# Broadcast of the expert combine weights: high and low part in the input products' one-pass format, in place of three bf16 parts

## What is computed

```python
g = jax.nn.sigmoid(xf @ gate_w.T)
topv, topi = jax.lax.top_k(g, K)                     # K = 4 of E = 16 experts
wn = topv / jnp.sum(topv, axis=-1, keepdims=True)
combine = jnp.zeros_like(g).at[jnp.arange(T)[:, None], topi].add(wn)
hin = jnp.einsum('td,edh->eth', xf, e_win)           # h = 64 per expert
vin = jnp.einsum('td,edh->eth', xf, e_vin)
h = silu(hin) * vin * combine.T[:, :, None]
routed = jnp.einsum('eth,ehd->td', h, e_wout)
shared = silu(xf @ ws_in) * (xf @ vs_in) @ ws_out
```

## Time and profile before

| | us |
|---|---|
| median of 3 runs | 918.67 |
| lowest, highest | 916.25, 920.44 |
| the profiled execution | 916.93 |
| its span | 915.2 |
| broadcast products, L1392: 128 | 49.4 busy, 386 ns each |
| transposes of the weights, L1382: 64 | 6.6 busy, 227 ns each |

### The profile page before, as it was taken

How to read it: one execution, slowest core, us unless ns; L and a number is a source line. 1 busy time by engine, 2 the same in 40 slices (tenths; PEclk the granted TensorE clock), 3 DMA queues, 4 the chain that set the end, 5 groups by cost and what they waited for, 6 DMA issues and landing times.

```text
span 915.2 us, 17726 instructions
## 1 busy us (share of the span) xinstructions
PE 823.2 (90%) x5783; PEld 643.9 (70%) x5783; DVE 669.4 (73%) x1759; ACT 363.3 (40%) x621; POOL 372.1 (41%) x372
## 2 busy tenths in 40 slices
PE   6879866799999999899989999999999999999966
PEld 5646655677777777777777777777777777777754
DVE  5899944577777777777786878777867777878654
ACT  4767742224343434333333443333434343433131
POOL 5040037253536262626262626353726353534200
PEclk8999977699999999999999999999999999999979
DMA  4877734300403040404030403040304040400000
GB/s 114 258 242 271 272 116 119 115 25 24 126 23 126 24 126 23 126 23 126 23 126 23 126 23 126 23 126 23 126 23 126 23 126 23 126 23 24 1 11 12
DMA packets 53104, 81.01 MB, mean 89 GB/s; under 512 B 10176, under 2 KB 36952, under 8 KB 49112
## 3 DMA queue, kind: packets, MB, share of 16 engines
q1 hardware_dynamic: 53080, 80.68, 28.2%
HBM read 55.24 MB, written 25.43 MB: 88 GB/s over the span
## 4 chain that ended last, share of the span: by engine, by line
PE 49%; DVE 17%; issue 14%; DMA 10%; POOL 5%; SPq 3%; ACT 2%; POOLq 1%; DVEq 0%; ACTq 0%
PE bank L1402 12%; DMA max_b<-max_scratch 7%; PE bank L1372 5%; PE bank L1376 5%; PE bank L1373 5%; PE bank L1392 4%; PE bank L1345 3%; DVE st L991 3%; PE bank L1321 3%; DVE acc L839 2%; PE bank L1319 2%; DVE Y L1003 2%; PE bank L1326 2%; DMA x_in<-in_L_attn_x_dram 2%; DVE out_sb L1003 2%
## 5 line engine op out<-in xcount | busy, mean ns | idle before, releaser
L755 ACT ACTIVATE s_in<-bank 128x512 f32<-128x512 f32 x144 | 85.9, 597 | 195.9 <-PE bank L1376 195.0
L1402 PE MATMUL bank<-ewout,h 128*128 128x128 f32 x1024 | 146.5, 286 | 0.0
L1402 PEld LDWEIGHTS bank<-ewout,h 128*128 128x128 f32 x1024 | 123.9, 191 | 25.4 <-issue 25.4
L554 POOL TENSOR_TENSOR rs<-ve,half 128x4 f32<-128x4 f32 x32 | 32.6, 1019 | 267.5 <-DVE ve L999 267.5
L1103 DVE TENSOR_TENSOR h<-s_in,bank 128x512 f32<-128x512 f32 x144 | 98.1, 681 | 58.5 <-PE bank L1376 50.3
L1372 PE MATMUL bank<-yT_hi,in_hi 128*128 128x512 f32 x288 | 128.2, 445 | 6.8 <-DVE h L1103 6.8
L1376 PE MATMUL bank<-yT_lo,in_hi 128*128 128x512 f32 x288 | 115.3, 400 | 0.0
L1373 PE MATMUL bank<-yT_hi,in_lo 128*128 128x512 f32 x288 | 114.6, 398 | 0.0
L540 POOL TENSOR_TENSOR D<-a_tok,max_b 128x512 f32<-128x512 f32 x64 | 65.4, 1043 | 118.5 <-DVE max_b L911 67.9
L1107 DVE TENSOR_TENSOR h<-h,bank 128x512 f32<-128x512 f32 x128 | 87.3, 682 | 19.8 <-PE bank L1392 19.8
L952 DVE TENSOR_TENSOR state<-kept,bank 64x130 f32<-64x130 f32 x128 | 36.6, 286 | 64.8 <-POOL kept L569 34.7
(11 more groups left out here) (197 smaller groups left out, 1634.2 us busy)
## 6 DMA issues: line engine op xcount, KB each, us to landing
xact_scratch<-xact SPq DMA_DIRECT2D x16, 1024.0 KB, 4.9
max_b<-max_scratch SPq DMA_DIRECT2D x15, 1024.0 KB, 7.7
xa<-xact_scratch SPq DMA_DIRECT2D x16, 512.0 KB, 6.4
silu_z<-xact_scratch SPq DMA_DIRECT2D x16, 512.0 KB, 3.8
inter_w<-inter_scratch SPq DMA_DIRECT2D x30, 256.0 KB, 7.0
x_in<-in_L_attn_x_dram SPq DMA_DIRECT2D x16, 256.0 KB, 4.9
xt_scratch<-x_t SPq DMA_DIRECT2D x16, 256.0 KB, 4.8
xT<-xt_scratch SPq DMA_DIRECT2D x16, 256.0 KB, 8.0
```

The costliest lines, as they stand in the source:

```text
L755: act.activation(s_in[:, j % 2], bank[4][:], ACT.Silu).then_inc(silu_done, 1)
L1402: i = pe.matmul(bank[7][:, k * P:(k + 1) * P], h2[:, j % 2, k * P:(k + 1) * P], w, start=(j == k == 0), stop=(j == NJ), skip_group_check=True)
```

## The change

The combine weights are split into two parts in fp32r, a high part and the rest (`comb2`: 16 + 16 columns for each chunk), in place of three in bf16. VectorE's five operations of part 3 become two: a cast and a subtraction. The transposes take `comb2` in fp32, 32 columns, and fill 32 partitions of bank 6 over all of its 512 columns. `combT` is fp32r with 128 partitions: ScalarE fills the first 32 in each pass, after a new wait for the last broadcast of the pass before, and the rest is set to zero once. `pair_rows` is fp32r with 128 rows, made in `pair_f` (two parts for three) and copied. The broadcast product is so an fp32r product on the full 128x128 array. `ident_bf` goes; the counts of the semaphores follow.

```diff
-        pair_rows = sb("pair_rows", [3 * NX, NJ, P], BF16)
+        pair_rows = sb("pair_rows", [P, NJ, P], F32R)
-        comb_r = sb("comb_r", [P, 2, NC, NX])
-        comb3 = sb("comb3", [P, NC, P // NX, NX], BF16)
-        combT = sb("combT", [3 * NX, G], BF16)
+        comb2 = sb("comb2", [P, NC, 2 * NX], F32R)
+        combT = sb("combT", [P, G], F32R)
...
-            halves = pair_rows[:].rearrange("r j (t m) -> r j t m", t=P // HX)
-            for part in range(3):
+            halves = pair_f[:].rearrange("r j (t m) -> r j t m", t=P // HX)
+            for part in range(2):
                 pool.affine_select(out=halves, in_=halves, compare_op=ALU.not_equal, fill=1.0, base=-NX * part,
                                    pattern=[[-2, NJ], [-1, 2], [0, HX]], channel_multiplier=1).then_inc(pool_const, 1)
                 pool.wait_ge(pool_const, CONSTS + 1 + part)
+            pool.tensor_copy(pair_rows[:], pair_f[:]).then_inc(pool_const, 1)
...
-            pool.memset(comb3[:], 0.0).then_inc(phase2_const, 1)
+            pool.memset(combT[:].bitcast(F32), 0.0).then_inc(phase2_const, 1)
...
                     act.wait_ge(combT_mm, f + 1)
-                    copy(combT[:], bank[6][0:3 * NX, 0:G // 2].bitcast(BF16)).then_inc(combT_out, 1)
+                    prev(act, bc_mm, f, NJ)
+                    copy(combT[0:2 * NX], bank[6][0:2 * NX, :]).then_inc(combT_out, 1)
...
                     after(9)
-                    dve.tensor_copy(comb3[:, :, 0], comb[:]).then_inc(route, 1)
+                    dve.tensor_copy(comb2[:, :, 0:NX], comb[:]).then_inc(route, 1)
                     after(10)
-                    dve.tensor_tensor(comb_r[:, 0], comb[:], comb3[:, :, 0], ALU.subtract).then_inc(route, 1)
-                    after(11)
-                    dve.tensor_copy(comb3[:, :, 1], comb_r[:, 0]).then_inc(route, 1)
-                    after(12)
-                    dve.tensor_tensor(comb_r[:, 1], comb_r[:, 0], comb3[:, :, 1], ALU.subtract).then_inc(route, 1)
-                    after(13)
-                    dve.tensor_copy(comb3[:, :, 2], comb_r[:, 1]).then_inc(route, 1)
+                    dve.tensor_tensor(comb2[:, :, NX:], comb[:], comb2[:, :, 0:NX].bitcast(F32), ALU.subtract
+                                      ).then_inc(route, 1)
...
                 for k in range(NC):
-                    i = pe.transpose(bank[6][:, k * P // 2:(k + 1) * P // 2].bitcast(BF16),
-                                     comb3[:, k].rearrange("p t e -> p (t e)"), ident_bf[:])
+                    i = pe.transpose(bank[6][0:2 * NX, k * P:(k + 1) * P], comb2[:, k].bitcast(F32), ident[:])
                 i.then_inc(combT_mm, 1)
```

More of the change, by code:

```diff
@@ L89, in mixer_moe_block @@
         ident = sb("ident", [P, P])
-        ident_bf = sb("ident_bf", [P, P], BF16)
         block_mask = sb("block_mask", [P, P])
         center = sb("center", [P, P])
-        pair_rows = sb("pair_rows", [3 * NX, NJ, P], BF16)
+        pair_rows = sb("pair_rows", [P, NJ, P], F32R)
         qkv_small = sb("qkv_small", [P, 3, NP, QD])
@@ L178, in mixer_moe_block @@
         in_w = sb1("in_w", [P, 2, NJ + 1, P])
+        pair_f = sb1("pair_f", [P, NJ, P])
         min_f = sb1("min_f", [P, HALVES, P])
@@ L484, in _ @@
             pool.memset(ident[:], 0.0).then_inc(pool_const, 1)
-            pool.memset(ident_bf[:], 0.0).then_inc(pool_const, 1)
             pool.memset(block_mask[:], 1.0).then_inc(pool_const, 1)
             pool.memset(center[:], -1.0 / DH).then_inc(pool_const, 1)
-            pool.memset(pair_rows[:], 0.0).then_inc(pool_const, 1)
+            pool.memset(pair_f[:], 0.0).then_inc(pool_const, 1)
             pool.memset(xm[:, 0, :, 0:HALO], 0.0).then_inc(pool_const, 1)
             pool.memset(g_pad[:], 0.0).then_inc(pool_const, 1)
[L491 to L494, removed]
+            pool.wait_ge(pool_const, 6)
+            pool.affine_select(out=ident[:], in_=ident[:], compare_op=ALU.not_equal, fill=1.0, base=0,
+                               pattern=[[-1, P]], channel_multiplier=1).then_inc(pool_const, 1)
             bm = block_mask[:].rearrange("p (b d) -> p b d", d=QD)
@@ L501, in _ @@
                                base=-DH, pattern=[[0, DH]], channel_multiplier=1).then_inc(pool_const, 1)
-            pool.wait_ge(pool_const, 12)
+            pool.wait_ge(pool_const, 10)
             pool.affine_select(out=bm, in_=bm, compare_op=ALU.is_ge, fill=0.0, base=QD - 1,
@@ L1494 @@
 U_SLOT = {0: 0, 1: 1, 2: 2, 3: 3}
-IDENT = 9
-CONSTS = 14
+IDENT = 7
+CONSTS = 12
 SCAN_DECAY = 10
@@ L1505 @@
 BACK = 3
-ROUTE = 14
+ROUTE = 11
 _INS = ['L0_attn_x', 'L0_attn_W_up', 'L0_attn_conv_w', 'L0_attn_conv_b', 'L0_attn_Wq', 'L0_attn_Wk', 'L0_attn_Wv',
```

## The result

| | before | after |
|---|---|---|
| median of the runs of this comparison, us | 919.56 (916.25 to 926.89, 4 runs) | 885.91 (881.61 to 889.50, 4 runs) |
| ratio, 95% interval | | 0.9637 [0.9592, 0.9682] |
| profiled execution, us | 916.93 | 881.61 |
| its span, us | 915.2 | 879.9 |

The change takes 33.6 us off the median of this comparison, 24.5 were forecast; 885.9 us is 2 us under the low end of the range. The sign and the place of the gain were as told, the size was not.

A forecast was written before the change was run, and what follows sets the result against it. Bound by TensorE, with max_b's transfer deciding eight of 16 passes up to the third broadcast. Gains of 8.0 us in (a), 14.9 in (b) and 1.6 in pass 15 make 24.5: 894.2 us, chance 0.58, range 888 to 908.

The forecast's parts named there:

- (b): From the third broadcast product to the next pass, set by TensorE: 22.39 us a pass, 14.9 us to be won.
- (a): Pass start to third broadcast, set by the later of TensorE's queue or max_b and GpSimd: 8.0 us to be won.
- Part 1: The 128 broadcast products in one-pass format on the full array lose the gaps around them: 0.18 us won each.
- Rival 5: The broadcast's one-pass load is exposed, nothing started ahead: 0.10 us more a broadcast, 925.6 us; chance 0.05.
- Part 2: VectorE's five small operations become two: 0.27 us won in undisturbed passes, 3.3 for four passes' collisions, 1.75 in pass 0.
- the 4.9 us for passes 2, 6, 10 and 14: Gain in (a) of these four passes: 1.6 us, plus 3.3 for VectorE's collisions with GpSimd's subtraction.
- Part 3: Four bf16 transposes of the weights a pass become fp32: 0.22 us dearer, plus 0.1 for a change of shape.
- Rival 2: The weights' transposes run at the full fp32 price, 0.45 us in 7 passes: 3 us, 897; chance 0.17.
- Part 4: ScalarE's copy and new wait, setup clears and masks: all 0; without cover the copy costs some 2 us once.
- Rivals 3 and 4: 3: one side of the broadcast gap closes, 903.8, chance 0.10. 4: gap stays, from waiting for h2, 914.3, chance 0.10.
- The last pass: Pass 15, without a mixer: 0.7 us sooner, dearer transposes -0.5, 8 broadcasts 1.4: 1.6 us won.
- a last pass that keeps its clock (1.2 us): Item for the low end of the range: pass 15 without the fall to 1.2 GHz, 1.2 us.

The follow-up runs named there:

- Experiment 9: Changed kernel with max_b issued early, ahead of the store, and GpSimd's first subtraction issued ahead of mixed[1], the second in slot 2: 865.97 us, ratio 0.9444.
- experiment 1: Kernel before with only the broadcast's shape changed: three bf16 parts kept, pair_rows and combT on 128 rows, the added ones zero: 885.81 us, ratio 0.9665.
- 7: Kernel of experiment 1 with the bf16 broadcast product over 80 rows instead of 128: 884.54 us, ratio 0.9657.
- experiment 8: Kernel of experiment 1 with the bf16 broadcast product over 64 rows instead of 128: 916.32 us, ratio 0.9999.
- experiment 2: Changed kernel with the one-pass broadcast product over only the 32 filled rows, a part of the array: 922.25 us, ratio 1.0058.
- 3: Kernel before with only the broadcast product in fp32r over 128 rows; three bf16 parts, five VectorE operations and bf16 transposes kept: 885.87 us, ratio 0.9649.
- experiment 5: Kernel of experiment 4 with GpSimd's first pair of subtractions moved from behind kept[1] to behind kept[0]: 877.85 us, ratio 0.9584.
- 6: Kernel of experiment 1 with the moves of experiment 4 and experiment 5 (early max_b, moved subtractions): 880.90 us, ratio 0.9640.
- experiment 4: Changed kernel with max_b issued right after load_z, ahead of the store of the finished group, 17 us sooner: 879.76 us, ratio 0.9568.

## Why the prediction was off, point by point

**What bounds the kernel: right in kind, wrong in share.** The reading in two halves held: (b) is TensorE's and constant to 0.02 us in passes 1 to 14 of each kernel, (a) is the later of two things. But the forecast took the passes that `max_b` sets as a fixed set of eight, with 22.80 to 26.37 us for (a) before and no number for the floor under them. After, (a) is 21.91 (passes 3 and 14) to 24.51, and the chain goes through `max_b` in twelve. Experiment 9 shows the floor that TensorE's own queue sets: 21.90. Of the 10.7 us won in (a), 1.95 are in pass 0 (1.9 forecast) and 8.7 in the other fourteen (6.1 forecast).

That agreement is worth little. The transfer is issued 6.3 us after the start of the pass in both kernels, so the change doesn't bring it forward, and GpSimd's start to the third broadcast is 9.26 us before and 9.20 after. What differs is how soon the transfer landed. In passes 2, 6 and 10 of before it landed early (GpSimd starts 11.2 to 11.5 us after the start of the pass), and the split set (a); in after it lands later there (14.1 to 15.3), and the three together win nothing (-0.2). In the other ten passes with a transfer GpSimd starts 6.8 us sooner in sum, and they win 7.7; pass 14, which has none, wins 1.2. Over all kernels with the transfer in its old place these starts spread alike, between 11.1 and 15.7 us, with no pattern that I found. In experiment 10, the changed kernel again, (a) is 352.1 us in sum: 8.4 under before, and not 10.7. How much of the 8.7 is the change's is open, and that 10.7 stands near 8.0 is luck in good part.

**Part 1, the price of a broadcast: the step that failed.** "0.65 - 0.46, with unrounded starts 0.18 us, is won" counted two distances. There are three. The 0.99 us of the eight fp32 records behind a broadcast stood in the trace of before (627.52 to 628.51, above), but the sum stops at the first of them, since the edit doesn't touch them: the undisturbed figure, 0.89 for eight records of 0.11, was taken as given. A broadcast was worth 0.29 and not 0.18. Net of the 0.10 that the pass loses at its end it is 1.49 / 5.5 = 0.27, and 0.09 x 5.5 x 15 is 7.4 us: 22.2 were won in (b) where 14.9 were forecast. That is the whole miss of (b), and most of the 9.1 us between 33.6 and 24.5. The third place shows in before as soon as the distances between L1402 records are set side by side: 0.213 us behind a broadcast, 0.112 elsewhere. The 0.10 that is lost has its place told wrong too: I named the `h` product of slot 7 as next late in (b), and it is the wait for `Y` at the end of the pass, which only the two-part split has.

The question that the forecast left open is settled: the rows, not the format (1, 7, 8). The Trainium skill (TensorEngine Tiling (Array Packing), Key Properties) says that a change of the tiling mode drains the engine. The rows of before and of experiments 7 and 8 agree that there is a price, 0.29 us for a lone product of 48 or 64 rows and none for 80; two thirds of it fall behind the product, a third even after the first record that follows.

**The load: right.** The one-pass load (0.19 us) stays under the product in front, started 0.23 us ahead. The rule of the Trainium skill that speaks against it (TensorE: Matmul & The Clock Gate, The mechanism: a load overlaps only with another row group) isn't borne out by after either: both have the same rows. Rival 5 is false for this kernel. Its mechanism shows in experiment 2 with the partial shape, 0.11 us a broadcast over before, where I had put 0.10.

**Part 2, VectorE: right and nearly worthless.** The waits for VectorE went from 11.2 to 2.6 us as told; the collision of pass 0 stayed, with the second operation as told (189.12, 1.01 us). Those of passes 2, 6 and 10 are gone; in this trace the transfer landed too late there to test it, but others do. In pass 8 of experiment 2, with two operations, GpSimd starts 11.05 us into the pass and finds the split done; in pass 2 of experiment 8, with five, it starts at 11.09, the last three take 1.06, 1.00 and 0.53 us, and the transposes come 2.3 us later than in the other (13.83 for 11.49). Pass 14 never had the collision, since it has no subtraction: its second operation took 0.53 us before and 0.52 after. But taking the operations away moved nothing in the time (3 against the changed kernel), since `max_b` lands behind it. A second step that failed is so the 4.9 us for passes 2, 6, 10 and 14: they won 1.0 together (-0.2 and 1.2), because the sum assumes that nothing is next late there. The split has a worth of 0.44 us a pass only with the transfer out of the way (5 against 6).

**Part 3, the transposes: cheaper than forecast.** The timeline of after, TensorE and then VectorE:

```profile
587.24 0.66 PE L1293 MATMUL bank<-ident,keyT 128*128 128x128 f32 x4
587.73 0.60 PE L1376 MATMUL bank<-ident,comb 128*32 128x128 f32 x4
588.09 0.47 PE L1366 MATMUL bank<-yT_hi,in_hi 128*128 128x512 f32 x1
...
586.88 0.20 DVE L1084 CAST comb<-comb 128x64 fp32r<-128x64 f32 x1
587.11 0.23 DVE L1086 TENSOR_TENSOR comb<-comb 128x64 fp32r<-128x64 f32 x1
```

L1293's four start at 587.24 and the next four at 587.73, with 0.109 us between any two records except the first pair; the input product follows 0.36 us after their start. From the first transposes to the input product it is 0.85 us, and it was 1.07 before (561.80 to 562.87): 0.22 won in a pass that TensorE sets, where the sum had 0.27 - 0.32, a loss of 0.05. The transposes cost 0.15 more than the bf16 ones, not 0.22, and the two changes of shape, 0.1 each in the sum, aren't there. Rival 2 (0.22 between two) is false. The Trainium skill (TensorEngine Tiling (Array Packing), Restrictions) says that column tiling disables the transpose mode for fp32; these transposes into 32 partitions keep the spacing of the full ones, so the trace does not show that rule at work. That phase 1 pays 0.32 us in front of products of 32 columns and this place doesn't isn't explained by any run here.

**Part 4: right.** No wait of ScalarE for the eighth broadcast shows in after, and its copy takes 0.59 us as before; the copy of the masks took 1.10 us where some 2 were put, all covered; pass 0 starts 0.5 us earlier, well within how much that start moves.

**Rivals 3 and 4: false**, by the 0.23 on both sides.

**The last pass** won 1.9 us where 1.6 were put. Its clock changes level several times, and not at the same places in each execution. The timeline of after, an input product ahead of the wait and the transposes behind it, and the same of experiment 10, the same kernel:

```profile
846.34 0.41 PE L1367 MATMUL bank<-yT_hi,in_lo 128*128 128x512 f32 x1
...
850.23 1.03 PE L1376 MATMUL bank<-ident,comb 128*32 128x128 f32 x4 [2.29 <-DVE comb L1086]
```

```profile
846.23 0.63 PE L1367 MATMUL bank<-yT_hi,in_lo 128*128 128x512 f32 x1
...
850.12 0.61 PE L1376 MATMUL bank<-ident,comb 128*32 128x128 f32 x4 [1.55 <-DVE comb L1086]
```

In after the granted clock is 0.91 between 846 and 848 us and 0.50 (1.2 GHz) between 850 and 852; in experiment 10 it is the other way round, 0.50 and then 1.00 (2.4 GHz). So experiment 10 doesn't keep its clock: it is slow for longer ahead of the wait, which makes the wait shorter, and is at the full clock behind it, where after falls a second time. The pass takes 40.23 us in after and 38.88 there. The item of the range, "a last pass that keeps its clock (1.2 us)", happens so from the transposes on, in part of the executions.

The range missed because it had no item for a third distance: it went 6 us below the forecast, for landings, the last pass and the spread of the runs, and 7.4 were missing from a term that had no range of its own.

## What to carry to other kernels

When one product with few rows stands alone among products of the full array, give it the full shape by zero rows (here 80 of 128 were enough, with 64 nothing was won): in experiment 1 the product itself took no longer (388 ns for 386), and an edit of a few lines won 32 us of 917. When such a thing is priced from a trace, measure from the last undisturbed product ahead to the first undisturbed one behind, past the instructions that the edit doesn't touch. And before a saving is booked in a stage, move the next-late thing away in a trial: here a transfer hid one part of the change, and once it was moved a collision of two engines hid much of the gain.

## What the runs showed of the hardware that was not expected

- The rows of a bf16 product that stands alone between full-array products have two prices as far as these runs go: 48 and 64 rows cost 0.29 us a product, 80 and 128 nothing. Part of it (0.213 us instead of 0.108) falls between the first and the second fp32 record after the product.
- A one-pass fp32r product of 32 rows costs 0.39 us more than one of 128 (experiment 2); its load of 0.18 us starts with it and not ahead.
- Five operations of VectorE on 128x64 that began beside an instruction of GpSimd on 128x512 lasted until 0.05 to 0.08 us behind that instruction's end: 503.11 for 503.06 and 504.14 for 504.06 in experiment 4, 411.53 for 411.48 in experiment 5, 579.76 for 579.68 in experiment 9 (a mask, L558), 656.54 for 656.49 in the earlier trace rows. So 0.18 to 0.23 us became 0.55 to 1.00, by what was left of GpSimd's instruction. Not every operation is held: the state updates, which read a bank of PSUM, took 0.28 to 0.29 us each beside the same subtractions and alone.
- The 1 MB transfer of `max_b`, issued 6.3 us into each pass right behind a store and the load of `x_res`, lands after 7.6 us in the median of after, and GpSimd starts 12.6 to 15.3 us after the pass starts. It decides most passes of the changed kernel and makes them unequal. Issued 17 us earlier and ahead of the store, it lands after 6.4 us (experiment 4), nothing waits for it from pass 1 on, and passes 1 to 13 are equal to 0.05 us.
